# Causal and first wide attention stage of a two-block transformer kernel in a new order of side work, with Newton steps in three turns and the first modulation on GpSimd

## What is computed

```python
mod = (silu(c) @ wmod).reshape(8, 6, 1, -1)           # sa, ca, ga, sb, cb, gb
ga, gb = sign(g) * maximum(abs(g), 0.25)              # for each of the two gates
h = layernorm(x) * (1 + ca) + sa                      # layer norm 0
x = x + ga * causal_attention(h)                      # 16 heads, x1 in the kernel
h = layernorm(x) * (1 + cb) + sb                      # layer norm 1, then modulated: ffn_x
xn = layernorm(h) * ln_g + ln_b                       # layer norm 2
o = full_attention(xn) @ wo + h                       # 32 heads
y = gelu(o_e @ w1[e] + b1[e]) @ w2[e] + b2[e]         # e = the expert of the half batch
out = x + gb * y
```

## Time and profile before

| | us |
|---|---|
| median of 3 runs | 1524.27 |
| lowest and highest | 1523.96, 1528.13 |
| profiled execution, whole | 1528.74 |
| its span, first to last instruction | 1526.7 |
| steps 0 to 47, causal stage | 169.9 of the span |
| steps 48 to 79, first wide stage | 116.0 of the span |

### The profile page before, as it was taken

One profiled execution on the slowest core, in us unless ns is written; L12 is line 12 of the kernel. 1 busy time (PEld: TensorE's weight loads), 2 busy tenths in 40 slices (PEclk: granted clock), 3 DMA queues, 4 the chain that ended last, 5 costly groups with the idle time before them and its releaser, 6 DMA issues.

```text
span 1526.7 us, 29704 instructions
## 1 busy us (share of the span) xinstructions
PE 1403.2 (92%) x9537; PEld 595.7 (39%) x9537; DVE 1143.9 (75%) x2889; ACT 994.3 (65%) x2074; POOL 485.3 (32%) x1217
## 2 busy tenths in 40 slices
PE   6689798799999999999999999999999989998998
PEld 5234242233434334343434334343344323342437
DVE  6577879898687887869687786878778697858621
ACT  1055466677667667776667666676767766767772
POOL 4145243334241334315332243413343133302100
PEclk9599899999999999999999999999999999999999
DMA  6856444347355453835645373654537242525230
GB/s 194 228 124 168 100 142 132 79 144 197 96 171 127 131 149 97 241 84 155 153 135 143 115 194 93 190 136 130 137 107 206 76 127 60 174 76 133 89 124 15
DMA packets 193886, 204.96 MB, mean 134 GB/s; under 512 B 58432, under 2 KB 143744, under 8 KB 193736
## 3 DMA queue, kind: packets, MB, share of 16 engines
q1 hardware_dynamic: 188072, 199.08, 47.8%
q10 hardware_dynamic: 5664, 3.98, 0.9%
HBM read 123.99 MB, written 79.02 MB: 133 GB/s over the span
## 4 chain that ended last, share of the span: by engine, by line
PE 71%; DVE 13%; ACT 7%; issue 3%; DMA 3%; SPq 2%; POOL 1%; DVEq 0%; ACTq 0%; POOLq 0%
PE bank_out L1519 17%; PE bank_scores L1497 13%; PE bank_max L1475 9%; PE bank_side L1436 8%; PE bank_side L1616 6%; DVE max_column L1760 5%; PE bank_max L1596 4%; PE bank_side L1449 3%; ACT probs L1294 3%; PE bank_side L1569 2%; PE bank_side L1596 2%; DVE bank_max L1757 2%; PE bank_side L1557 2%; PE bank_scores L1596 2%; PE bank_side L1411 1%
## 5 line engine op out<-in xcount | busy, mean ns | idle before, releaser
L1294 ACT ACTIVATE probs<-bank_scores 128x512 f32<-128x512 f32 (+3 forms) x1536 | 752.4, 543 | 286.1 <-PE bank_scores L1497 280.2
L1760 DVE TENSOR_REDUCE max_column<-bank_max 128x1 f32<-128x512 f32 x1024 | 653.1, 683 | 106.6 <-PE bank_max L1475 102.0
L1519 PE MATMUL bank_out<-probs,v_tile 128*9 128x512 f32 (+4 forms) x3072 | 364.8, 547 | 4.4 <-issue 1.7
L1475 PE MATMUL bank_max<-k_stack,q_stack 64*128 64x512 bf16 (+3 forms) x2048 | 313.0, 342 | 42.6 <-DVE max_column L1757 14.2
L1497 PE MATMUL bank_scores<-q_stack,k_stack 64*128 64x512 bf16 (+3 forms) x2048 | 315.0, 344 | 35.0 <-ACT probs L1294 34.3
L1757 DVE CUSTOM_DVE_ANT_0 bank_max<-bank_max,causal 128x384 f32<-128x384 f32 (+3 forms) x512 | 241.6, 514 | 103.0 <-PE bank_max L1475 100.9
L1497 PEld LDWEIGHTS bank_scores<-q_stack,k_stack 64*128 64x128 bf16 x2048 | 80.9, 93 | 417.5 <-issue 410.5
L1148 POOL CAST max_parts<-max_row 128x32 bf16<-128x32 f32 x96 | 23.0, 240 | 436.5 <-DVE max_row L1773 436.0
L1475 PEld LDWEIGHTS bank_max<-k_stack,q_stack 64*128 64x128 bf16 x2048 | 104.1, 95 | 116.9 <-issue 78.8
L1616 PE MATMUL bank_side<-w_out,hidden_T 128*128 128x256 f32 x448 | 126.6, 405 | 0.0
L1166 POOL TENSOR_SCALAR_AFFINE_SELECT probs<-probs 128x512 f32<-128x512 f32 x128 | 81.5, 637 | 58.6 <-ACT probs L1294 58.6
(11 more groups left out here) (162 smaller groups left out, 1351.1 us busy)
## 6 DMA issues: line engine op xcount, KB each, us to landing
q_stack<-q_parts SPq DMA_DIRECT2D x124, 256.0 KB, 4.5
k_stack<-k_parts SPq DMA_DIRECT2D x124, 192.0 KB, 6.0
out_raw<-out_raw SPq DMA_DIRECT2D x74, 256.0 KB, 2.1
w_in<-in_L_ffn_w_dram SPq DMA_DIRECT2D x15, 1024.0 KB, 5.1
w_out<-in_L_ffn_w_dram SPq DMA_DIRECT2D x15, 1024.0 KB, 8.4
q_parts<-partsq SPq DMA_DIRECT2D x32, 384.0 KB, 2.7
k_parts<-partsk SPq DMA_DIRECT2D x32, 384.0 KB, 2.8
q_parts<-partsq SPq DMA_DIRECT2D x32, 256.0 KB, 3.1
```

The lines of the kernel that those rows point to most:

```text
L1294: nc.scalar.activation(probs[s % 2][:, head_at(k), q0:S], region[bank][:, q0:S], ACT.Exp, scale=float(WIDTH[a]) ** -0.5).then_inc(drained[ ...
L1475: ins = pe.matmul(region[to][:, 0:keys], q_stack[buf][rows, at, qt * P:(qt + 1) * P], k_stack[buf][rows, at, 0:keys], start=(i == 0), stop ...
L1519: ins = pe.matmul(outb[32 * k:32 * k + WIDTH[a] + 1, q0:S], v_tile[a][:, kt, g * GROUP + k, :], probs[s % 2][:, k, q0:S], start=(kt == 0), ...
L1760: v.tensor_reduce(dst, region[bank], AX_X, ALU.max).then_inc(drained[bank], 1)
```

## The change

The change writes no new arithmetic. It has five parts.

1. **Newton steps in three turns.** For the layer norms (2, 0), (0, 1), (0, 2) and (3, 0) piece 6 does only the first 5 of the 13 steps, and two new items `newton` do four each, a step of attention apart. All Newton steps are now on GpSimd; DVE does none.
2. **The first modulation on GpSimd.** `scale_and_modulate` is gone. DVE writes `normed` for (0, 1) as for other batches, and GpSimd's `ffn_input` modulates it, one tile of four at a time.
3. **Side work in a new order.** In the causal stage the units stand further apart. Layer norm (3, 0) moves from steps 68 to 72 into steps 34 to 39, and its `to_features` from step 73 to steps 46 and 47. The eight `qk` units of batch 3 move from steps 74 to 79 to steps 48 to 58; the four `v` units of batch 3 move from the first pass (steps 80 to 86) to steps 59 to 61; the four `attention_out` of batch 2 move from steps 83 to 85 to steps 78 to 81, and with them `bias_part` of batch 1 from step 81 to step 72. The `qk` units of batch 1's wide block come three to four steps later. Batch 0's `ffn_sum` and its last `scale_heads` come up to two steps later.
4. **Causal stacks behind rows of maxima.** The `stacks` of the causal stage move by a few slots; those of batch 1 now stand behind the store of the rows of maxima. In the first wide stage `stacks` (1, 2) moves from step 67 to step 69.
5. **`keep_x`** (a 128x1024 copy on ScalarE) moves from the 18th to the 20th step in each of five passes, steps 97 to 99 in the first.

```diff
+NEWTON_APART = ((2, 0), (0, 1), (0, 2), (3, 0))
...
-    place_units(plan, first, (172,), [("keep_x", n)])
+    place_units(plan, first, (193,), [("keep_x", n)])
...
-    place(plan, 77, [("stacks", 1, 2)])
+    place(plan, 85, [("stacks", 1, 2)])
...
-    place(beside, 12, [("stacks", 1, 0)])
+    place(beside, 18, [("stacks", 1, 0)])
...
+    place_at(beside, (91, 95), [("newton", 0, 1, 1), ("newton", 0, 1, 2)])
+    place_at(beside, (99, 102, 103, 107), [("ffn_input", 0, t) for t in range(T_STEPS)])
...
             def ffn_input(b, f, half):
-                for t in range(2 * half, 2 * half + 2):
-                    wait(pool, normed_made[1], T * (b - 1) + t + 1)
+                tiles = range(half, half + 1) if b == 0 else range(2 * half, 2 * half + 2)
+                for t in tiles:
+                    wait(pool, normed_made[1], T * b + t + 1)
                     pool.tensor_tensor(ffn_x[:, t, :], normed[1][:, t, :], mod_bc[:, 1, :], ALU.mult).then_inc(ffn_scaled, 1)
...
             def layernorm(b, f, n, piece):
-                if piece == NEWTON_PIECE and not (b == 0 and n):
-                    for step in range(GUESS_STEPS, ROOT_STEPS):
+                if piece == NEWTON_PIECE:
+                    last = GUESS_STEPS + 5 if (b, n) in NEWTON_APART else ROOT_STEPS
+                    for step in range(GUESS_STEPS, last):
                         newton_step(pool, b, n, step)
+
+            def newton(b, f, n, turn):
+                for step in range(GUESS_STEPS + 1 + 4 * turn, GUESS_STEPS + 5 + 4 * turn):
+                    newton_step(pool, b, n, step)
...
-            def scale_and_modulate(half):
-                for t in range(2 * half, 2 * half + 2):
-                    v.scalar_tensor_tensor(out=ffn_x[:, t, :], in0=x1[:, t, :], scalar=mean_var[:, 1, t, 0:1],
...
-                    if b == 0 and n:
-                        for step in range(GUESS_STEPS, ROOT_STEPS):
-                            newton_step(dve, b, n, step)
+                    pass
```

88 lines of the change are left out of this document (43 added, 45 removed).

## The result

The changed kernel takes **1517.72 us** (median of five, 1514.32 to 1519.81) against 1524.27 for the kernel before (five, 1523.96 to 1528.24). The ratio is 0.9943 with a 95% interval of 0.9922 to 0.9964, that is 5.5 to 11.9 us less. I had forecast 1506.8 and a range of 1497 to 1517: the direction was right, the gain a third to two thirds of what I had claimed, and the median 0.7 us outside the range. The profiled execution took 1518.21 with a span of 1516.3, 10.4 less than the span before.

What follows compares the result with a forecast made beforehand. PE was taken as 71% of the chain of waits, DVE 13%, with DVE setting some stretches. Terms -3.8 (causal stage), -2.0, -4.7, -6.5 and -0.5 sum to -17.5, from 1524.27 to 1506.8 us; range 1497 to 1517.

Steps and rivals of the forecast that it cites:

- Newton off DVE: Steps 24 to 31: Newton steps and modulation leave DVE, 34.1 to 26.7 us, -7.4, bounds -9 and -3.
- I take nothing for it: No charge for masks queued behind GpSimd's added pieces: cover about a step, 3.3 us, against 2.9 for the longest piece.
- Steps 16 to 23, 32 to 39, 40 to 47: Rest of the causal stage: -1.4 for three units lost, +2.8 for layer norm (3, 0), +2.6 for added units.
- Steps 0 to 15: Start of the causal stage, 57.3 us: same units spaced better, layer norm (2, 0) earlier, -0.4, bounds -3 and +3.
- Steps 48 to 63: First wide stage, set by DVE: added units, fewer waits behind `to_features`, 60.3 to 58.3 us, -2.0, bounds -4 and +2.
- Steps 64 to 79: Second half of the wide stage, PE's: 55.7 to 51.0 us, -4.7, with 1.0 charged for batch 1's tight stack.
- Steps 80 to 89: Start of the first pass: units leave, 45.7 to 39.2 us, -6.5, bounds -8 and -4.
- `keep_x`: Copy on ScalarE in five passes: 0.1 us gained each, -0.5, bounds -2.5 and +1.
- the causal stage gives nothing: Rival: layer norm (3, 0) costs its full 3.9 us and stacks come late; 1513 us, chance 0.25.
- work is only moved: Rival: added units turn DVE-bound steps PE-bound, waits reappear at the first pass's experts; 1522 us, chance 0.07.
- GpSimd becomes the bound: Rival: Newton turns queue behind masks and DVE waits at `normed`, slower; 1531 us, chance 0.05.
- it gives more: Rival: even spacing takes another 8 us of PE's 20.4 us idle in the causal stage; 1498 us, chance 0.12.

Runs made afterwards that it cites:

- the run without turns: Changed kernel, all places kept, but the 13 Newton steps of the four causal norms in one row on GpSimd: 1524.7 us, ratio 0.9986 to the kernel before.
- the one with the places of before: Kernel before, order kept, with Newton steps of norms (0, 1), (0, 2) in one row and (0, 1)'s modulation on GpSimd: 1528.44 us, ratio 1.0024.
- the run with the `ffn_sum` parts: Changed kernel with five repairs (stack, values, `bias_part`, step 69's stack, inverse with scaling) and first-pass `ffn_sum` parts ahead of the last `expert_in`: 1509.94 us, ratio 0.9887.
- the value units alone: Changed kernel with batch 1's value units back at slots 15, 19, 27, 31 and its causal stack left at slot 18: 1516.46 us, ratio 0.9939.
- the one with stack at 12 and value units late: Changed kernel with batch 1's causal stack back at slot 12 and its value units at 15, 19, 27, 31: 1513.33 us, ratio 0.9922.

## Why the prediction was right and wrong

- **Newton off DVE (-7.4 forecast, -8.2 measured): right, mechanism and size.** The rate of the next stretch was the right measure, the clock came back, and GpSimd's added work stayed hidden. Two of the numbers under it were off: DVE's busy time fell by 5.4 us and not by 7.5, in part since a row of 13 steps holds DVE for 2.5 us but is busy for 2.1, and since the second pair of `normed` took 1.25 us beside GpSimd; and GpSimd was busy for 15.05 us and not 22, since the first norm's Newton steps came ahead of step 24 and no `qk` split was left in the stretch. The runs add that part of the gain held only with turns; "I take nothing for it" was right by the margin of the turns.
- **Steps 16 to 23, 32 to 39, 40 to 47 (+4.0 forecast for the three, +2.5 measured): right**, each within 0.5.
- **Steps 0 to 15 (-0.4, measured +2.8): the step that failed.** I had priced "the same units spaced better" at nothing and looked for a danger in batch 1's first maxima. The loss was at the load of the rows. I had seen that it stood behind eight issues and "perhaps behind their data", but not who waits: before the change the chain ended at 104.35 and PE arrived at 104.18, and so waited for only 0.17 us, because a value unit of 1.13 stood ahead. Moving that unit for spacing removed the cover, and putting the stack between store and load, which my -0.4 took to be harmless, cost as much again: 2.2 and 2.3 of the 4.5 us in steps 4 to 11. The trace of before had that row; I didn't read PE's arrival there. My upper bound of +3 did hold it.
- **Steps 48 to 63 (-2.0, measured +0.3).** Of the miss of 2.3, DVE's busy time is 1.0 (54.80 for my 53.75: both pairs of `normed` stretched beside GpSimd, and two more maxima in the window) and its idle time the rest (5.8 for my 4.8, and the 0.2 for the clock). DVE's waits for maxima, of which I had struck out 4.6, fell from 5.1 to 2.1. The wait for `bias_part` grew by 0.55 us where I had 0.9, but putting it back gave 1.1 on the path.
- **Steps 64 to 79 (-4.7, measured -3.9).** The tight stack was foreseen at 1.0 with a bound of 2.6; it was 1.87.
- **Steps 80 to 89 (-6.5, measured -3.1): the other step that failed, a term mis-sized.** The eight steps 80 to 87 measured 24.4 for my 22.5. Steps 82 to 86 took 2.8 on average and not 2.65, which is 0.8 of it, and step 80 took 3.85 and not 3.12: PE stands still in it for 0.83 us, as it already did before the change (0.84), and I hadn't read that row. The 8.0 that I expected for taking six units out also contradicts my own price of 0.4 to 0.6 for a unit, by which they give 2.4 to 3.6. They gave 3.4, and that 6.2 came is luck: the rest is the wait for the inverse that left the stretch, and one `ffn_sum` part fewer in it. Steps 88 and 89 cost +3.0 for my +1.5: one more `ffn_sum` (1.1) and waits of 1.2 and 0.9 that the new order of `scale_heads` and of the last part makes.
- **`keep_x` (-0.5): measured -0.9**, some 0.2 a pass, so the term was right to half a microsecond.
- **From span to median.** I took the same difference for both. The profiled execution of before was one of its long ones, 4.5 above its median; that of the changed kernel was 0.5 above its own. So the spans differ by 10.4 us, the medians by 6.6, and the ratio over all executions gives 8.7.

Of the rivals, the result lies between "the causal stage gives nothing" (1513) and "work is only moved" (1522), and is neither: the causal stage gave 2.9 of my 3.8, by a larger gain and an unforeseen loss, and the moved units saved 3.4 us for 2.0 paid. "GpSimd becomes the bound" did not happen, but the run without turns, and the one with the places of before, showed its waits. The rival "it gives more" has a slip in its sum: 17.5 and 8 us off 1524.3 are 1498.8.

What stays open: in five of fourteen profiles of kernels with the stack at slot 85 steps 72 to 75 took 16.2 to 16.6 us and in the others 14.0 to 14.8, with edits that don't touch them. The longer ones show the lower clock; why the same wait of some 2 us sometimes brings it and sometimes not, the runs don't tell. A wait of 1.53 us was followed by the lower clock (the run with the `ffn_sum` parts), one of 2.31 was not (the value units alone). It is open too whether the modulations in a row would cost anything once the Newton steps come in turns.

## What to carry to other kernels

Before a unit of work is moved for the sake of even spacing, read when its engine arrives at the next thing it needs from a DMA: a unit right ahead of such a point is its cover, and 1.1 us of it was worth 2.2 here, 4.5 together with the stack's order. Work handed to an idle engine must be cut so that no piece is longer than the slack of what queues behind it; the same instructions in one row took back 6.6 us of steps 20 to 39. In a queue that one engine issues, count the chains that must land in the same window, since their order only chooses which of them is late.

## What the runs showed of the hardware

A small transfer issued behind a stack's eight took more than twice as long: the store of the maxima rows 3.1 us alone and 7.2 to 8.2 behind the stack, their load 1.9 and 6.9, the store of the inverse 7.3 to 7.9 behind a stack, landing 0.2 to 0.3 us after the stack's last.

GpSimd's modulations kept 0.71 to 0.83 us where two of DVE's `normed` beside them went from 0.73 to as much as 1.66: there DVE lost. It is not always DVE. An instruction of GpSimd's split of the maxima that took 0.24 us elsewhere took 0.88 when it began while DVE's `normed` was still under way and the scaling of the heads came right behind:

```profile
244.60 0.24 POOL L1159 TENSOR_TENSOR max_row<-max_row,max_parts 128x32 f32<-128x32 f32 x1
...
290.09 0.70 DVE L1708 TENSOR_SCALAR normed<-normed,mean_var,rstd 128x256 f32<-128x256 f32 x2
290.61 0.88 POOL L1159 TENSOR_TENSOR max_row<-max_row,max_parts 128x32 f32<-128x32 f32 x1
290.70 0.69 DVE L1807 TENSOR_TENSOR heads_T<-heads_T,inverse_T 128x512 f32<-128x512 f32 x1
```

It ended at 291.49, 0.1 us after DVE's scaling.

A lower clock comes and goes at places that no edit touched. The last 64 steps hold the same instructions in the same order in all these kernels; two of them, from step 320 to the end (the changed kernel, and the one with stack at 12 and value units late):

```profile
1230.10:1516.31 286.21, 263.08 (x1530) 117.56 (x1528) 172.45 (x321) 189.43 (x361) 50.46 (x130) 0.99 0.33 98
```

```profile
1224.70:1508.29 283.59, 260.25 (x1530) 115.83 (x1528) 172.51 (x321) 189.45 (x361) 50.40 (x130) 1.00 0.34 98
```

They differ by 2.6 us and by a hundredth of the clock. Together with the start of step 0, which moves by up to 3.8 us between the profiles, that comes near to what the change itself gained, and is the reason why a term of 1 us is read from a stretch, not from a median.
